# WKV recurrence of an RWKV block: running mean and log weight in place of numerator, denominator and division

## The reference, cut to what matters

```python
def _wkv(w, u, k, v):
    def step(carry, kv_t):
        aa, bb, pp = carry
        kt, vt = kv_t
        ww = u + kt
        p = jnp.maximum(pp, ww)
        e1 = jnp.exp(pp - p)
        e2 = jnp.exp(ww - p)
        y = (e1 * aa + e2 * vt) / (e1 * bb + e2)
        ww2 = pp + w
        p2 = jnp.maximum(ww2, kt)
        e1 = jnp.exp(ww2 - p2)
        e2 = jnp.exp(kt - p2)
        return ((e1 * aa + e2 * vt, e1 * bb + e2, p2), y)
...
sr = sigmoid(xr @ Wr.T);  w = -exp(time_decay);  att = _wkv(w, time_first, k, v)
x = x + (sr * att) @ Wo.T
```

## Time and profile before

| | us |
|---|---|
| median of 3 runs | 1274.45 |
| the 3 runs | 1271.92, 1274.45, 1278.95 |
| span of the profiled execution | 1283.2 |
| busy PE / PEld / DVE / ACT / POOL | 1090.3 / 863.1 / 1010.1 / 580.8 / 644.2 |

### The profile page before, as it was taken

The page is one execution under the profiler, slowest core; times in us unless marked ns, Lnnn a source line. Parts: engine busy times, 40 slices in busy tenths (PEclk is TensorE's granted clock), DMA queues, the critical chain, the costliest instruction groups (busy, mean ns, idle before and its releaser), DMA issues.

```text
span 1283.2 us, 19742 instructions
## 1 busy us (share of the span) xinstructions
PE 1090.3 (85%) x5152; PEld 863.1 (67%) x5153; DVE 1010.1 (79%) x1969; ACT 580.8 (45%) x1021; POOL 644.2 (50%) x547
## 2 busy tenths in 40 slices
PE   4579989498978889897898858888978999999997
PEld 4257777366656566665666545765767888888886
DVE  3899996989989898999989996888932566666654
ACT  1436646263635555364554435472632333333332
POOL 3437565352434325243442466867753565555553
PEclk9869989799999899999999979898988999999999
DMA  9233330101101010110101010104023333333220
...
DMA packets 60055, 80.45 MB, mean 63 GB/s; under 512 B 7774, under 2 KB 47327, under 8 KB 60002
## 3 DMA queue, kind: packets, MB, share of 16 engines
...
## 4 chain that ended last, share of the span: by engine, by line
PE 33%; DVE 28%; issue 18%; POOL 11%; ACT 6%; DVEq 1%; SPq 1%; DMA 1%; ACTq 0%; another core or an unknown queue 0%; POOLq 0%
PE psM L965 10%; PE psKV L897 6%; PE psR L976 4%; PE psM L976 4%; PE psM L848 4%; DVE bnst L1271 3%; POOL cf L410 2%; DVE mix_lo L1316 2%; POOL sorted_list L400 2%; ACT arena L550 2%; PE psT L801 2%; PE psT L955 2%; DVE arena L1324 2%; DVE s_ring L1386 2%; DVE arena L1294 1%
## 5 line engine op out<-in xcount | busy, mean ns | idle before, releaser
L897 PE MATMUL psKV<-arena 128*128 128x256 f32 x1024 | 255.4, 407 | 2.8 <-ACT arena L625 1.4
L897 PEld LDWEIGHTS psKV<-arena 128*128 128x128 f32 x1024 | 209.7, 208 | 43.2 <-issue 8.8
L430 POOL TENSOR_SCALAR arena<-arena,vecs 128x512 f32<-128x512 f32 x64 | 77.9, 1225 | 212.3 <-DVE arena L1289 212.1
L836 PE MATMUL psM<-arena 128*128 128x512 f32 x384 | 175.5, 607 | 9.0 <-DVE arena L1294 4.6
L550 ACT ACTIVATE arena<-s_ring,cf 128x256 f32 (+1 forms) x128 | 66.4, 590 | 247.3 <-POOL cf L412 247.3
L965 PE MATMUL psM<-arena 128*128 128x128 f32 x1152 | 145.6, 280 | 0.1
L501 POOL DMA_INDIRECT out_dram<-arena,out_idx x72 | 91.4, 1269 | 101.9 <-DVE row_idx L1444 77.2
L965 PEld LDWEIGHTS psM<-arena 128*128 128x128 f32 x1152 | 136.9, 195 | 4.3 <-issue 1.9
L836 PEld LDWEIGHTS psM<-arena 128*128 128x128 f32 x384 | 72.4, 194 | 91.6 <-issue 83.9
L801 PE MATMUL psT<-cst,arena 128*128 128x128 f32 x256 | 46.5, 341 | 102.0 <-ACT arena L550 102.0
L711 ACT ACTIVATE arena<-arena,info_t 128x256 f32<-128x256 f32 x72 | 43.2, 600 | 169.7 <-DVE info_t L1449 155.9
...
## 6 DMA issues: line engine op xcount, KB each, us to landing
...
out_dram<-arena,out_idx POOLq DMA_INDIRECT x72
```

The source lines that it names most:

```text
L836: ins = pe.matmul(psM[:, u % 3, :], w[:, k, c * P:(c + 1) * P], mixA[:, m, k, :], start=(k == 0), stop=(k == CH - 1))
L897: ins = pe.matmul(psKV[:, j // 2, (j % 2) * C:(j % 2 + 1) * C], kf2[:, h, j * P:(j + 1) * P], wfv[:, h, :], start=(h == 0), stop=(h == HC ...
```

## The change

With `l` the logarithm of the sum of weights and `y` the weighted mean, the recurrence becomes: the scan over the sum of weights stays (now into `lb`); ACT takes its Ln; DVE adds it to the difference `qb`, which gives the log ratio between past weight and new weight; ACT takes tanh of half of it, once with the decay as bias and once with `time_first` as bias; a second scan keeps the running mean `y`, and the output is a mix of `y` and `v` by the second tanh. Gone are the second exponent pair (`uneg`), the numerator scan, the products, the sum and the reciprocal. Factors of 2 are folded into `wo` (0.125 in place of 0.5). `exps` now takes both chunks in one instruction pair at the head of ACT's round; `logs` stands after ReLUs 0 to 2 and `shares` (the tanh) after ReLUs 3 to 5; ReLUs 6 and 7 and all eight squares stand behind them. On DVE `wkv_state` stands ahead of `extra` 0, `residual2`, `moments1` and `fetch`; then come `wkv_gap`, `extra` 1 and `wkv_mix`.

```diff
--- before.py
+++ after.py
@@ -39,7 +39,7 @@
 LIST_ROUND = SELECT_ROUND + 1
 RING = 6
 R_PEXP, R_COUNTS, R_SEL, R_ONEHOT, R_KEPT, R_ALL = 9, 13, 18, 30, 31, 54
-WKV_STEPS = 24
+WKV_STEPS = 16
 PARAMS = ["ln1_w", "ln1_b", "ln2_w", "ln2_b", "decay", "first", "tmk", "tmv", "tmr", "cmk", "cmr"]
 
 
...
@@ -139,14 +140,13 @@
         mixA = part(3 * CH * SEQ).rearrange("p (m c t) -> p m c t", m=3, c=CH)
         dmix = part(CH * SEQ).rearrange("p (c t) -> p c t", c=CH)
         kvs = part(3 * CH * SEQ).rearrange("p (m c t) -> p m c t", m=3, c=CH)
-        E1 = [part(2 * SEQ).rearrange("p (m t) -> p m t", m=2) for _ in range(CH)]
-        E2 = [part(2 * SEQ).rearrange("p (m t) -> p m t", m=2) for _ in range(CH)]
+        E1 = part(CH * SEQ).rearrange("p (c t) -> p c t", c=CH)
+        E2 = part(CH * SEQ).rearrange("p (c t) -> p c t", c=CH)
         qb = [part(SEQ) for _ in range(CH)]
         kx = part(CH * SEQ).rearrange("p (c t) -> p c t", c=CH)
-        evb, t1b = kx[:, 0], kx[:, 1]
         pp = [part(SEQ + 1) for _ in range(CH)]
-        aa = part(SEQ + 1)
-        bb = part(SEQ + 1)
+        lb = [part(SEQ + 1) for _ in range(CH)]
+        yy = [part(SEQ + 1) for _ in range(CH)]
         att = part(CH * SEQ).rearrange("p (c t) -> p c t", c=CH)
         hT = part(CH * (SEQ + 1)).rearrange("p (c t) -> p c t", c=CH)
         hn = part(J * C).rearrange("p (j c) -> p j c", j=J)
@@ -219,6 +219,7 @@
         probs_turned routed pads_out list_cur list_scattered list_in w1_in w2_in
         x_in x_out s_out fetched x0_ready scaled0 embedded moments_step ln1_stats cf1_ready hn1_ready tr1_done
         h1_ready mix1_step mix1_done mixr_scaled mixr1_done proj_done kvr_ready wkv_step pre_done relu2_done exp_done att_done o_done
+        state_done log_done gap_done past_done now_done
         x2_done ln2_step ln2_stats cf2_ready hn2_ready tr2_done h2_ready mix2_step mixk_done mixk_hi wfk_hi_done mix2_done mixr2_done
         kf_done relu_done sq_done fr_done sigf_done kv_done s_done s_mult rstd1_step rstd2_step
         rows_zeroed idx_ready s_idx_ready info_ready xn_done turned mlp_in_ready h_done gelu_done y_done tanh_done
@@ -599,14 +600,29 @@
             def exponents(b, c):
 
                 wait_run(act, S["pre_done"], b * CH + (c + 1))
-                act.activation(E2[c][:, 0], qb[c], ACT.Relu, bias=wneg[:, c:c + 1])
-                act.activation(E2[c][:, 1], qb[c], ACT.Relu, bias=uneg[:, c:c + 1]).then_inc(S["relu2_done"], 1)
-
-            def exps(b, c):
-
-                act.activation(E1[c], E1[c], ACT.Exp).then_inc(S["exp_done"], 1)
-                wait_run(act, S["relu2_done"], b * CH + (c + 1))
-                act.activation(E2[c], E2[c], ACT.Exp, scale=-1.0).then_inc(S["exp_done"], 1)
+                act.activation(E2[:, c], qb[c], ACT.Relu, bias=wneg[:, c:c + 1]).then_inc(S["relu2_done"], 1)
+
+            def exps(b):
+
+                act.activation(E1, E1, ACT.Exp).then_inc(S["exp_done"], 1)
+                wait_run(act, S["relu2_done"], b * CH + CH)
+                act.activation(E2, E2, ACT.Exp, scale=-1.0).then_inc(S["exp_done"], 1)
+
+            def logs(b):
+
+                for c in range(CH):
+                    wait_run(act, S["state_done"], b * CH + (c + 1))
+                    act.activation(lb[c][:, 1:SEQ + 1], lb[c][:, 1:SEQ + 1], ACT.Ln).then_inc(S["log_done"], 1)
+
+            def shares(b):
+
+                for c in range(CH):
+                    wait_run(act, S["gap_done"], b * CH + (c + 1))
+                    act.activation(E1[:, c], qb[c], ACT.Tanh, scale=-0.5, bias=half_w[:, c:c + 1]
+                                   ).then_inc(S["past_done"], 1)
+                for c in range(CH):
+                    act.activation(E2[:, c], qb[c], ACT.Tanh, scale=-0.5, bias=half_u[:, c:c + 1]
+                                   ).then_inc(S["now_done"], 1)
 
             def split_mix(b, c):
 
@@ -642,15 +658,16 @@
                     square(b, h)
 
             def round_(b, ffn=True, ahead=True, softmax=False, further=True):
+                exps(b)
                 if ffn:
-                    exponents(b, 1)
-                    relus(b - 1, 0, 1)
-                    exps(b, 1)
-                    relus(b - 1, 2, 3)
-                    for h in range(4, HC):
-                        squares(b - 1, h - 4)
-                        relus(b - 1, h)
-                    squares(b - 1, *range(HC - 4, HC))
+                    relus(b - 1, 0, 1, 2)
+                logs(b)
+                if ffn:
+                    relus(b - 1, 3, 4, 5)
+                shares(b)
+                if ffn:
+                    relus(b - 1, 6, 7)
+                    squares(b - 1, *range(HC))
                 if softmax:
                     act.wait_ge(S["route_exp_in"], 1)
                     act.activation(probs, logits, ACT.Exp).then_inc(S["route_exp_out"], 1)
@@ -666,14 +683,11 @@
                 norm2(b)
                 if ahead:
                     take_kvr(b + 1, 2, 4)
-                if ahead:
-                    exponents(b + 1, 0)
                 affine2(b)
                 for c in range(CH):
                     if ahead:
                         take_kvr(b + 1, 4 + c, 5 + c)
-                        if c == 0:
-                            exps(b + 1, 0)
+                        exponents(b + 1, c)
                     split_mix(b, c)
 
             norm0(0)
@@ -681,12 +695,9 @@
             act.wait_ge(S["weights_in"], 16 * 4)
             act.activation(wfk_hi[:], wfk, ACT.Copy).then_inc(S["wfk_hi_done"], 1)
             affine1(0)
-            take_kvr(0, 0, 2)
+            take_kvr(0, 0, 4)
             exponents(0, 0)
-            exps(0, 0)
-            take_kvr(0, 2, 4)
             exponents(0, 1)
-            exps(0, 1)
             norm0(1)
             take_kvr(0, 4, 6)
             round_(0, ffn=False)
@@ -998,17 +1009,19 @@
             v.memset(hT[:, :, 0:1], 0.0)
             for c in range(CH):
                 v.memset(pp[c][:, 0:1], -1e38)
-            v.memset(aa[:, 0:1], 0.0)
-            v.memset(bb[:, 0:1], 0.0).then_inc(S["columns_set"], 1)
+                v.memset(lb[c][:, 0:1], 0.0)
+                ins = v.memset(yy[c][:, 0:1], 0.0)
+            ins.then_inc(S["columns_set"], 1)
             v.wait_ge(S["columns_set"], 1)
 
             def prepare():
                 v.wait_ge(S["decay_exp"], 1)
+                v.tensor_scalar(half_w[:], wneg[:], 0.5, None, ALU.mult)
                 v.tensor_scalar(wneg[:], wneg[:], -1.0, None, ALU.mult)
-                v.tensor_scalar(uneg[:], vecs[:, :, V["first"]], -1.0, None, ALU.mult)
+                v.tensor_scalar(half_u[:], vecs[:, :, V["first"]], 0.5, None, ALU.mult)
 
                 v.wait_ge(S["weights_in"], 16 * 4)
-                v.tensor_scalar(wo.rearrange("p k n -> p (k n)"), wo.rearrange("p k n -> p (k n)"), 0.5, None, ALU.mult)
+                v.tensor_scalar(wo.rearrange("p k n -> p (k n)"), wo.rearrange("p k n -> p (k n)"), 0.125, None, ALU.mult)
                 v.tensor_scalar(wfv.rearrange("p k n -> p (k n)"), wfv.rearrange("p k n -> p (k n)"), 0.5, None,
                                 ALU.mult)
 
@@ -1329,54 +1342,75 @@
 
                 for c in range(CH):
                     st.wait(3 + c)
-                    v.tensor_scalar(E1[c][:, 0], qb[c], wneg[:, c:c + 1], 0.0, ALU.add, ALU.min)
-                    v.tensor_scalar(E1[c][:, 1], qb[c], uneg[:, c:c + 1], 0.0, ALU.add, ALU.min).then_inc(S["pre_done"], 1)
-
-            def wkv_end(b, c, st):
-
-                e1, f1, e2, f2 = E1[c][:, 0], E1[c][:, 1], E2[c][:, 0], E2[c][:, 1]
-                val, r = kvs[:, 1, c, :], kvs[:, 2, c, :]
-                v.wait_ge(S["exp_done"], b * (2 * CH) + (2 * c + 2))
-                v.wait_ge(S["kvr_ready"], b * (3 * CH) + (CH + c + 1))
-                weighted = st.then(v.tensor_tensor(evb, e2, val, ALU.mult))
-                state_b = st.then(v.tensor_tensor_scan(bb[:, 1:SEQ + 1], e1, e2, 0.0, ALU.mult, ALU.add))
-                st.wait(weighted)
-                state_a = st.then(v.tensor_tensor_scan(aa[:, 1:SEQ + 1], e1, evb, 0.0, ALU.mult, ALU.add))
-                st.then(v.tensor_tensor(t1b, f2, val, ALU.mult))
-                st.wait(state_b)
-                past_b = st.then(v.tensor_tensor(qb[c], f1, bb[:, 0:SEQ], ALU.mult))
-                st.wait(state_a)
-                past_a = st.then(v.tensor_tensor(e1, f1, aa[:, 0:SEQ], ALU.mult))
-                st.wait(past_b)
-                below = st.then(v.tensor_tensor(qb[c], qb[c], f2, ALU.add))
-                st.wait(past_a)
-                above = st.then(v.tensor_tensor(e1, e1, t1b, ALU.add))
-                st.wait(below)
-                st.then(v.reciprocal(e2, qb[c]))
-                v.wait_ge(S["kvr_ready"], b * (3 * CH) + (2 * CH + c + 1))
-                st.wait(above)
-                st.then(v.scalar_tensor_tensor(e1, r, 1.0, e1, ALU.add, ALU.mult))
-                st.wait()
```

(81 more changed lines are left out.)

3 lines of the change are left out of this document (2 added, 1 removed).

## The result

The changed kernel takes 1295.97 us (median of four runs, 1294.21 to 1301.38), the kernel before, on the same chip, 1276.7 (1271.92 to 1284.71). The ratio is 1.0144, with a 95% interval of 1.0096 to 1.0192. In a later group of runs it was 1.0082 (1.0050 to 1.0115). So the change makes this kernel about 1% slower; 1265 us, a ratio of 0.991, had been forecast.

The account below looks back on a forecast made before the run. DVE was taken to set the pace, PE close behind. Round terms −7.2 − 3.5 − 5.4 + 4.5 − 1.0 + 2.5 = −10.1 us gave 1273.1 off the span, 1264.4 off the median: 1265 us, 8-in-10 range 1240 to 1289.

Parts of the forecast that it names:

- Rounds 1 and 2 hold statistics in each slot and gain as much as they lose: 0.: Rounds 1 and 2, with statistics in each slot: gains and losses balance, 0 us.
- 54.4: −0.9, eight times: Common rounds 4 to 11: each falls from 55.3 to about 54.4 us, −7.2 us in all.
- The clock: Rival, PE: new idle gaps bring the low clock, 0.8 us per `channel_out`, +10 in 12 rounds: 1275 us; chance 0.27.
- The loads: ACT, each round: two table loads for Ln and tanh, 1.28 us each, the first hidden, the second not.
- The rival's 2.21: Rival, ACT's second load: at 2.21 us, 0.93 later in 16 rounds, +15: 1280 us alone; within the slower case, 0.21.
- ACT's queue costs more than DVE gives back: Rival, ACT's second load: slower, 1290 us with load and clock, 1280 load alone; band 1281 to 1295, chance 0.21.
- Round 15: Last round: no `turn1` hides the late squares; three `channel_out` and `project_out` end 2.5 us later.
- Round 12: `place_tokens` on DVE stands behind two scans held up by POOL's `embed`; list, `rstd1` and `turn1` 4.5 us later.
- Rounds 0 and 3: Round 0, `att` earlier by DVE's work, later by ACT's: −3.5 us; round 3, L1386 earlier: −5.4 us.
- DVE's busy time: Sign that the forecast is right: DVE busy down by 170 us or so.
- the relief comes through: Rival: load absent or ahead of the wait, POOL not holding the scans; about 4 us in 12 rounds, 1217 to 1240; 0.07.

Follow-up runs that it names:

- The gap first on DVE: Changed kernel with `wkv_gap` moved ahead of `moments1` and `fetch` on DVE: 1266.58 us, ratio 0.9874 to the kernel before.
- the tail ahead of the tanh: Changed kernel with ReLUs 6 and 7 and all eight squares ahead of the tanh on ACT, DVE's order unchanged: 1200.78 us, ratio 0.9333 to the kernel before.

## Why the prediction was wrong, step by step

The forecast was −10.1 us, and the spans rose by 11.2: 21.3 us of miss that the rounds must explain. The other 10 us between 1265 and 1296 are no mechanism: the profiled execution of before, at 1284.71 us, lay 10.3 above the median of 1274.45 from which the forecast started, and that of after lay at its own median.

**The failed step: "Rounds 1 and 2 hold statistics in each slot and gain as much as they lose: 0."** They lost 15 us, more than the whole difference between the spans (11.2). The step counted DVE's instructions and did not walk the round. Two moves that the diff shows meet there. `moments1` now stands ahead of the gap, and in these rounds it waits for POOL's `embed`, until 113.56 us in round 1, because POOL has its share of the statistics (9.8 us) ahead of `embed`. The ReLUs and squares now stand behind the gap. The gap first on DVE took 19 us off these two rounds, and the tail ahead of the tanh, with the wait left as it was, also made round 1 short. I had walked the whole chain for a common round and named who is queued behind ACT's wait, but never asked in which rounds what ends that wait comes late, though the row of before (119.51, idle 1.85) was there to read.

**Common rounds, "54.4: −0.9, eight times".** The plain ones took 54.83, but the eight together changed by +1.8 and −0.3 us instead of −7.2. Two terms were mis-sized, on opposite sides. The gap was walked to be out at t 11.9; it began at 13.7 and came at 14.4, as `extra` 0 took 3.4 us instead of 1.7 (one instruction of it stood for 1.95 beside POOL's L424 where its twin takes 0.18), and the statistics copy 1.03 (0.17 in the run with the gap first) beside POOL's L446. So the squares ended at t 23.5 (21.0 forecast) and x2 came at 39.0 (36.3). Against it, `mix_lo` 1 no longer met POOL's L434: x2 to the end of `mix_lo` took 54.83 − 39.0 = 15.8 us, 18.1 forecast. Eight plain rounds thus give 8 x (54.83 − 55.3) = −3.8 us. The rest, +5.6 and +3.5, sits in single longer rounds, of which each profile has two to four, and there it is mostly the clock.

**The clock.** That PE's idle time would move from ahead of `turn1` to ahead of `receptance` and `channel_out` was right; that it was free ahead of `turn1` was not quite, since `channel_out` 2 behind it took 4.45 us and more, and `project_out` came right behind. Its price was no term of the sum: I had it as a rival at +0.8 a round, +10 in all, and took it as absent. In a plain round it was absent from the path: half of `receptance` took 3.47 to 3.68 us instead of 1.89, but still ended before the squares, and `channel_out` 0 took 3.69. In rounds 4, 8 and 11 the low clock went on and `channel_out` 0 took 6.00, 6.10 and 5.63. Round 8:

```profile
522.64 3.78 PE L896 MATMUL psM<-arena 128*128 128x256 f32 x8 [3.98 <-ACT arena L637]
527.37 6.10 PE L908 MATMUL psKV<-arena 128*128 128x256 f32 x16 [0.95 <-ACT arena L641]
```

6.10 − 3.69 = 2.4 us is just what this round (57.25) has above a plain one. The kernel before has such rounds as well, with the price behind its own wait ahead of `turn1`: in round 6 (56.56 us) `channel_out` 2 took 5.74 us where the earlier trace rows has 4.45.

```profile
421.19 5.74 PE L897 MATMUL psKV<-arena 128*128 128x256 f32 x16
```

So the rival's mechanism was there, but as some 2 us in three of the eight rounds, in both profiles of after, and not as 0.8 in each. What decides which round pays is not shown.

**The loads.** 32, at 1.28 us each, the first hidden, the second on the path: right, and the run without Ln gives 0.9 to 1.3 us a round. The rival's 2.21 was not seen; in a common round tanh starts 1.29 us after its load does. The rival "ACT's queue costs more than DVE gives back" was right in sign and place. It was short in reach (1280 to 1290, its band to 1295, against 1296), and its price, a dearer load, was wrong: from the gap to the last square the common round took the 9.1 us that were walked (14.4 to 23.5, walked 11.9 to 21.0). What costs is what is queued behind, and by the waits ahead of it, not by the load.

**Round 15**, +2.5 forecast, +7.4 and +3.8 measured; three `channel_out` in a row took 12.3 us after a wait of 2.64 instead of about 3 x 3.6. With the tail ahead of the tanh the round takes 46.8. **Round 12**, +4.5 forecast, −2.5 measured: the two scans ahead of `place_tokens` did not delay it as walked. No run was made for it, and it stays open. **Rounds 0 and 3** went as forecast in sign, a few us apart in size. **DVE's busy time** fell by 127.5, not 170: the new scans stand beside `embed` as the old ones did (5.22 us for two that take 2.3 alone); over the kernel the 32 of L1351 took 72.7 us, some 35 more than alone.

**The rival "the relief comes through"** asked for a hidden load or no POOL in the way. Neither is the condition. With the loads there and POOL as it is, the order on ACT alone brings 1200.8 us. That is below the range given even to this rival (1217 to 1240), which was walked with PE's waits shortened by 4 us, not gone.
